# A scan beside two expert layers on one core: load queue in block order, scan input loaded twice, delta one tile sooner

## The chip, the cores and the metric

One core of a Trainium2 chip runs the whole program. The metric is the device time of one execution in microseconds. Before the change it is 2816.26 us, the median of three runs (2815.76, 2816.26 and 2824.55 us).

## The reference

The input x is (2, 2048, 1024) in float32, so 4096 rows of 1024 channels. Cut to what matters:

```
def ffn(x):      # 64 experts of rank 16, top 4
    vecs  = einsum('arh,bsh->bsar', A, x)
    idx   = top_k(norm(vecs), 4);  routes = one_hot(idx).sum(-2) / 4
    v     = einsum('bsa,bsar->bsr', routes, vecs)
    delta = einsum('bsa,ajr,bsr->bsj', routes, B, v)
    return x @ W.T + bias + delta
def scan(x):     # selective scan, 16 states
    xz = x @ W_xproj.T;  delta_r, B_mat, C_mat = xz[..., :128], xz[..., 128:144], xz[..., 144:]
    delta = softplus(delta_r @ W_dt.T + b_dt)
    dA, Bu = exp(delta * A), delta * B_mat * x
    h = dA * h + Bu   (over time);   y = sum(h * C_t)
    return y + x * D_param
x = x + 0.5 * ffn(layernorm(x))
x = x + scan(layernorm(x))
x = x + 0.5 * ffn(layernorm(x))
```

## The kernel before

**Units.** The rows are cut into 32 row blocks of 128. A unit is one expert layer on one row block; kind 1 is the first layer (its result also feeds the scan), kind 2 is the second layer, which first adds the scan's y. There are 64 units, 0 to 63, and every engine runs its own program through them in the same order. `plan` mixes the kinds: 0 to 13 are kind 1, then both kinds in turn, from 48 on all are kind 2. In a unit TensorE does the 128-deep products of W (`base`), B (`routed`) and, for the next unit, A (`experts`). VectorE picks the experts, adds up and does the scan; ScalarE does the copies, the norms and the exponentials. In this text a unit begins where VectorE starts the MAX8 of line 1095.

**The scan beside it.** The scan is cut into 64 tiles of 128 channels by 512 time steps, or of 256 channels by 256 time steps where the chunk has two row blocks, in chunks of 4, 4, 8, 8, 8, 8, 8, 8, 4 and 4 tiles. A tile has 4 groups, a group has 4 blocks, so a tile has 16 blocks and there are 1024. One block is one ACTIVATE Exp on ScalarE (`decay`, line 934, writes pA, two buffers) and one TENSOR_TENSOR_SCAN on VectorE (line 1147). GpSimd multiplies each group by B before its scan (`times_b`, lines 506 and 512, two groups ahead of the scan) and by C behind it (`times_c`, line 522). TensorE sums the states (`sum_states`, line 721), and VectorE adds x times D (`sum_up`, line 1157). Units 3 to 59 carry 17 or 18 blocks each. `scans(lo, hi)` and `decays(lo, hi)` place them in the unit in twentieths; ScalarE's decays stand two blocks ahead.

**Delta.** For each tile TensorE makes z (`z`, line 702), ScalarE the softplus (lines 888 to 898), VectorE adds and multiplies by the scan's input x in xt (`delta`, lines 1128 and 1133), and ScalarE writes delta and delta times x to DRAM (line 912). `zs` of a unit says at which of three positions this stands. From DRAM the SP queue spreads both over the partitions, 512 KB in each of four transfers for a tile: `spread_inputs` (line 360) brings delta times x, halves 0 and 1, into Ur, for `times_b`; `spread_delta` (line 353) brings delta, halves 0 and 1, into Dr, for `decay`. Both rings hold three halves. Block n = 2 of a tile is the first that reads half 1 of Dr.

**The SP queue.** SP issues every load and store but those of line 912, in program order, and a wait of one holds all behind it. In a unit (`unit`, lines 430 to 470) the order is: `slot` 0, the tile load `load_tile` of position 0 (line 390), the load of the next unit's x (line 341), the store of the scan input (442), the two DMA transposes of `turn` (403), `slot` 1 and 2, `load_tile` of position 1, the stores of ranks and B, C (450, 451), `slot` 3 and 4, `load_y` (335) and the store of the result (466). A slot is a group. At the third group of tile t the slot has `store_tile(t - 1)`, which waits for `sum_up`, then both halves of `spread_inputs(t + 1)` and half 0 of `spread_delta(t + 1)`; at the fourth group it has half 1 of `spread_delta(t + 1)`. xt has three slots; a tile's x stays there from its load until y, written in its place, is stored. `load_tile(t)` waits for the store of tile t - 3. z of tile t stands six groups before the tile's own.

Of the kernel before, what the change touches and what calls it, by code (L numbers as in the profile page):

```python
# [4 lines left out]
P = 128  # L5
# [50 lines left out]
def plan(NF, CH):  # L56

    NGRP = CH[-1].group1
    NSL = NGRP + 3
    chunk_of_row = [c for c in CH for _ in range(c.rows)]  # L60
    first_tile = {c.tile0: c for c in CH}
    slot_unit, first = {}, 0
    for u in range(SCAN0, SCAN1):
        last = (u + 1 - SCAN0) * NGRP // (SCAN1 - SCAN0)
        for n in range(first, last):
            slot_unit[n] = (u, n - first)
        first = last
# [24 lines left out]

    NTL = CH[-1].tile1
    prev = (0, 0)
    for t in range(NTL):
        s = 4 * t - 6
        u, i = slot_unit[s] if s >= 0 else (SCAN0 - 1, 3)
        at = (SCAN0 - 1, 2) if t == 0 else (u, 0) if i == 0 else (u, 1) if i < 3 else (u + 1, 0)
        assert at > prev, (t, at, prev)
        if t in first_tile:  # L100
            f = f1_at[first_tile[t].row1 - 1]
            assert at[0] >= f + 2 or (at[0] == f + 1 and at[1] == 2), (t, at, f)
        us[at[0]].zs[at[1]] = t
        prev = at
    f1s = f2s = zs = 0
    for a, b in zip(us, us[1:] + [None]):
        a.after = b
        f1s += a.kind == 1
        f2s += a.kind == 2
        zs += len(a.zs)  # L110
        a.f1s, a.f2s, a.z_end = f1s, f2s, zs
    return us


def build(nc, x, AT, BT, WT, bias, WxT, WdtT, b_dt, A_log, D_par, out):
# [41 lines left out]
    with ctx:  # L157
# [107 lines left out]

        s_ldr = sem("s_ldr")
        s_ldb = [sem(f"s_ldb{n}") for n in range(4)]; s_ldc = [sem(f"s_ldc{n}") for n in range(4)]
        s_ldt = [sem(f"s_ldt{n}") for n in range(NXT)]; s_sty = [sem(f"s_sty{n}") for n in range(NXT)]
        s_ldd = [sem(f"s_ldd{n}") for n in range(NPR)]; s_ldu = [sem(f"s_ldu{n}") for n in range(NPR)]
        s_z = sem("s_z"); s_l = sem("s_l"); s_du = sem("s_du"); s_dc = sem("s_dc")  # L270
        s_dA = sem("s_dA"); s_sc = sem("s_sc"); s_sv = sem("s_sv"); s_bm = sem("s_bm"); s_cm = sem("s_cm")
# [10 lines left out]

            return 16 * (channels_at(i // 16) + part) + i % 16

        def rows_of(t):

            return xt[:, t % NXT, :].rearrange("p (u k t) -> p k u t", k=chunk_of_tile[t].parts, t=P)

        def split(a, c):

            return a.rearrange("p (k t) -> p k t", t=c.width)

        def slot_of(a, n):
            return a.slots[n] if n < len(a.slots) else None

        def block_at(a, twentieths):

# [3 lines left out]
        def _(sp):  # L301
# [26 lines left out]
            def load_y(b, a):  # L328
                if b.kind == 2:
                    row = b.v * P  # L330
                    sp.wait_ge(s_out, a.u * 2 + 2)
                    for n in range(NXT):
                        sp.wait_ge(s_sty[n], 16 * len(range(n, chunk_of_row[b.v].tile1, NXT)))
                    src = yT_d[row:row + P, :].rearrange("p (k t) -> p k t", t=P)
                    sp.dma_start(auxy, src).then_inc(s_ldy, 16)

# [44 lines left out]
                c, k = chunk_of_tile[t], channels_at(t)  # L381
                return d[:, c.row0:c.row1, k:k + c.parts, :].rearrange("p u k t -> p u (k t)")

            def tile_of(t):
                return xt[:, t % NXT, :].rearrange("p (u n) -> p u n", u=chunk_of_tile[t].rows)

            def load_tile(t):
                sp.wait_ge(s_stn, 16 * chunk_of_tile[t].row1)
                sp.wait_ge(s_sty[t % NXT], 16 * (t // NXT))
                sp.dma_start(tile_of(t), blocks_of(xnT_u, t)).then_inc(s_ldt[t % NXT], 16)  # L390

            def store_tile(t):
                sp.wait_ge(s_y, t + 1)
                sp.dma_start(blocks_of(yT_u, t), tile_of(t)).then_inc(s_sty[t % NXT], 16)

            def turn(a, y_done):

# [4 lines left out]
                    src = un2[:, part, :, :].rearrange("p k q -> p (k q)")  # L402
                    sp.dma_start_transpose(uT[:, part, :, :], src).then_inc(s_uc[part], 16)

            def slot(a, n):
                G = slot_of(a, n)
                if G is None:
                    return
                t = G // 4 + 1
                if G % 4 == 2:  # L410
                    if t >= 2:
                        store_tile(t - 2)
                    if t < NGRP // 4:
                        spread_inputs(t, 0)
                        spread_inputs(t, 1)
                        spread_delta(t, 0)
                if G % 4 == 3 and t < NGRP // 4:
                    spread_delta(t, 1)
                for c in CH[1:]:
                    if c.group0 - 4 <= G < c.group0:  # L420
                        spread_b(c, G - c.group0 + 4)
                    if c.group0 - 2 <= G < c.group0 + 2:
                        spread_c(c, G - c.group0 + 2)
# [5 lines left out]

            def unit(l, a, b):  # L430
                late = l if l and l.kind == 1 else None
                if 0 not in a.zs:
                    ranks_due(a, 1)
                slot(a, 0)
                if 0 in a.zs:
                    load_tile(a.zs[0])
                    ranks_due(a, 1)
                if b:
                    load_x(b, a)
                if late:  # L440
                    sp.wait_ge(s_nc, late.w * 2 + 2)
                    sp.dma_start(xnT_d[late.w * P:(late.w + 1) * P, :], auxs[:, :]).then_inc(s_stn, 16)
                turn(a, a.f2s + (b is not None and b.kind == 2))
                slot(a, 1)
                slot(a, 2)
                if 1 in a.zs:
                    load_tile(a.zs[1])
                if late:
                    sp.wait_ge(s_pc, late.w + 1)
# [8 lines left out]
                slot(a, 3)  # L458
                slot(a, 4)
                if b:  # L460
                    ranks_due(b, 0)
# [558 lines left out]
        def _(dve):  # L1020
# [102 lines left out]
            def delta(a, pos):  # L1123
                if pos not in a.zs:
# [5 lines left out]
                dve.wait_ge(s_ldt[t % NXT], 16 * (t // NXT + 1))  # L1130
                c = chunk_of_tile[t]
                by_rows = "p (k u t) -> p k u t"
                V.tensor_tensor(dd[:, 1, :].rearrange(by_rows, k=c.parts, t=P), pz.rearrange(by_rows, k=c.parts, t=P),
                                rows_of(t), ALU.mult).then_inc(s_du, 1)

            def scan(i):
                G, s = i // 4, i % 4
# [159 lines left out]
```

## Time and profile before

| | |
|---|---|
| median of three runs | 2816.26 us |
| profiled execution, its own time | 2817.88 us |
| its span in the profile | 2816.1 us |
| PE busy | 2600.7 us (92%) |
| POOL busy | 2349.3 us (83%) |
| DVE busy | 2221.5 us (79%) |
| ACT busy | 1497.5 us (53%) |
| moved by DMA | 373.50 MB, 133 GB/s |

PE is TensorE, PEld its weight loads, DVE is VectorE, ACT is ScalarE, POOL is GpSimd, SP is the queue that issues most DMAs; a q behind an engine's name is its sequencer. Busy is the time in which an engine has an instruction in work. The idle time before an instruction is put down to what released it, written `<-`. DMA times run from issue to landing.

### The profile page before, as it was taken

The numbers are of one execution on the slowest core, as the hardware profiler recorded it, in microseconds if no ns is written. First come the engines' busy times: TensorE is split into PE (matmuls) and PEld (weight loads), VectorE is DVE, ScalarE is ACT, GpSimd is POOL, SyncE is SP. The second block draws the span as 40 slices with busy tenths as digits, with TensorE's granted clock in tenths as the row PEclk, the third lists the DMA queues.
The fourth block names the chain that finished last, engine by engine and source line by source line (L and its number), as shares of the span: only waits on it lengthen the run. The fifth ranks groups of instructions, "written<-read, shape, count | busy, mean of one in ns | idle before, by whom it ended". The sixth has DMA issues, their size and how long they took to land.

```text
span 2816.1 us, 39802 instructions
## 1 busy us (share of the span) xinstructions
PE 2600.7 (92%) x13597; PEld 1177.0 (42%) x13664; DVE 2221.5 (79%) x2933; ACT 1497.5 (53%) x3363; POOL 2349.3 (83%) x703
## 2 busy tenths in 40 slices
PE   4988999999999999999999999999999998889999
PEld 1444444444344443444444434444344443444444
DVE  8447888888788887888878878788788887888843
ACT  5346666665555645556455555565555554655521
POOL 2138889989899898998999999999899999989910
PEclk8999999999999999999999999999999999999999
DMA  5144434544354443544544445444455434454321
GB/s 218 48 116 136 142 118 135 163 144 138 108 159 143 133 138 109 159 144 128 143 138 132 144 138 160 133 127 131 145 156 157 143 117 138 131 147 139 92 63 53
DMA packets 303520, 373.50 MB, mean 133 GB/s; under 512 B 148435, under 2 KB 220243, under 8 KB 303318
## 3 DMA queue, kind: packets, MB, share of 16 engines
q1 hardware_dynamic: 286422, 337.40, 40.2%
q10 hardware_dynamic: 16896, 33.56, 4.0%
q8 instruction: 108, 1.77, 0.3%
q14 instruction: 94, 0.77, 0.1%
HBM read 234.05 MB, written 103.29 MB: 120 GB/s over the span
## 4 chain that ended last, share of the span: by engine, by line
PE 24%; DVE 18%; ACT 5%; DMA 5%; DVEq 4%; issue 4%; SPq 1%; ACTq 1%; POOL 1%; POOLq 0%
DVE mreg L1147 10%; PE pv L554 8%; PE po L554 5%; PE pv L558 4%; PE po L558 3%; ACT pA L934 2%; PE py L721 2%; DMA delta_scratch<-mreg 2%; DVE pv L1108 1%; DVE sel L1105 1%; DVEq L1113 1%; DMA mreg<-xnT_scratch 1%; DVEq L1107 1%; DMA xin<-x_scratch 1%; DVE xin L1071 1%
## 5 line engine op out<-in xcount | busy, mean ns | idle before, releaser
L522 POOL TENSOR_TENSOR mreg<-mreg 128x2048 f32<-128x2048 f32 x256 | 1161.6, 4538 | 48.8 <-ACT hst L920 48.7
L1147 DVE TENSOR_TENSOR_SCAN mreg<-pA,hst,mreg 128x512 f32<-128x512 f32 (+1 forms) x1024 | 1043.8, 1066 | 103.0 <-ACT pA L934 72.9
L512 POOL TENSOR_TENSOR mreg<-mreg 128x1024 f32<-128x1024 f32 x340 | 795.4, 2364 | 234.1 <-DMA mreg<-delta_scratch 229.9
L934 ACT ACTIVATE pA<-mreg,nA 128x512 f32<-128x512 f32 (+1 forms) x1280 | 738.3, 596 | 452.6 <-DVE mreg L1147 403.3
L554 PE MATMUL pv<-wA,xT 128*128 128x512 f16 x2016 | 463.8, 382 | 52.3 <-ACT xT L841 41.7
L554 PE MATMUL po<-wB,uT 128*128 128x512 f16 x2016 | 470.4, 380 | 10.2 <-DVE xin L1071 7.2
L554 PE MATMUL po<-wW,xT 128*128 128x512 f16 x2016 | 470.9, 381 | 3.6 <-issue 0.2
L506 POOL TENSOR_TENSOR mreg<-mreg 128x2048 f32<-128x2048 f32 x86 | 390.0, 4535 | 2.0 <-issue 2.0
L554 PEld LDWEIGHTS pv<-wA,xT 128*128 128x128 f16 x2016 | 191.8, 98 | 335.7 <-ACT xT L841 90.2
L554 PEld LDWEIGHTS po<-wB,uT 128*128 128x128 f16 x2016 | 191.8, 98 | 273.3 <-issue 47.0
L554 PEld LDWEIGHTS po<-wW,xT 128*128 128x128 f16 x2016 | 196.0, 98 | 238.3 <-issue 24.8
L721 PE MATMUL py<-mreg,Em 128*32 128x512 f32 (+1 forms) x2560 | 274.6, 519 | 10.4 <-DVE mreg L1157 7.8
L1089 DVE TENSOR_REDUCE n<-sel 128x32 f32<-128x512 f32 x128 | 86.2, 674 | 236.8 <-ACT sel L849 236.7
L1147 DVE TENSOR_TENSOR_SCAN mreg<-pA,cst,mreg 128x256 f32<-128x256 f32 (+1 forms) x256 | 243.1, 999 | 21.1 <-ACT pA L934 18.0
L558 PE MATMUL pv<-wA,xT 128*128 128x512 f16 x1008 | 242.9, 385 | 17.4 <-DVE xT L1085 17.4
L558 PE MATMUL po<-wB,uT 128*128 128x512 f16 x1008 | 241.1, 382 | 0.0
L558 PE MATMUL po<-wW,xT 128*128 128x512 f16 x1008 | 238.7, 380 | 0.0
L849 ACT ACTIVATE sel<-pv 128x512 f32<-128x512 f32 x128 | 75.8, 593 | 203.4 <-PE pv L558 199.3
L558 PEld LDWEIGHTS pv<-wA,xT 128*128 128x128 f16 x1008 | 97.7, 99 | 148.3 <-issue 36.6
L558 PEld LDWEIGHTS po<-wW,xT 128*128 128x128 f16 x1008 | 96.5, 98 | 133.3 <-issue 21.3
L558 PEld LDWEIGHTS po<-wB,uT 128*128 128x128 f16 x1008 | 97.1, 99 | 125.6 <-issue 25.4
L1121 DVE SCALAR_TENSOR_TENSOR xin<-po,sc,xin 128x512 f32<-128x512 f32 x128 | 92.4, 722 | 59.9 <-PE po L558 56.7
(132 smaller groups left out, 2376.0 us busy)
## 6 DMA issues: line engine op xcount, KB each, us to landing
mreg<-delta_scratch SPq DMA_DIRECT2D x256, 512.0 KB, 5.9
delta_scratch<-mreg ACTq DMA_DIRECT2D x128, 256.0 KB
xin<-x SPq DMA_DIRECT2D x32, 512.0 KB, 3.6
x_scratch<-xin SPq DMA_DIRECT2D x32, 512.0 KB, 6.1
xnT_scratch<-auxs SPq DMA_DIRECT2D x32, 512.0 KB, 2.9
mreg<-xnT_scratch SPq DMA_DIRECT2D x64, 256.0 KB, 6.7
yT_scratch<-mreg SPq DMA_DIRECT2D x64, 256.0 KB, 2.5
uT<-yT_scratch SPq DMA_DIRECT2D x32, 512.0 KB, 4.5
```

Of the source, the lines that this page charges most:

```text
L506: pool.tensor_tensor(h, u, b.broadcast_to([P, 4 * c.parts, c.width]), ALU.mult).then_inc(s_bm, 2)
L512: pool.tensor_tensor(h[:, half * n:half * n + n, :], u, b.broadcast_to([P, n, c.width]), ALU.mult).then_inc(s_bm, 1)
L522: pool.tensor_tensor(h, h, by_c, ALU.mult).then_inc(s_cm, 1)
L554: last = nc.tensor.matmul(dst, lhs[:, 0, k, :], w[:, wb, k, nb * HF:(nb + 1) * HF], start=(first and k == 0 and wb == 0), stop=False)
L558: last = nc.tensor.matmul(dst, lhs[:, 1, k, :], w[:, 0, k, nb * HF:(nb + 1) * HF], start=False, stop=(stop and k == KD - 1))
L721: last = nc.tensor.matmul(split(py[32 * s:32 * s + 32, :], c)[:, n, :], Em[:, :], h[:, c.parts * s + n, :], start=(g == 0 and n == 0), sto ...
L849: nc.scalar.activation(sel[:, nb * HF:(nb + 1) * HF], pv[:, nb, :], ACT.Square).then_inc(s_sq, 1)
L934: last = nc.scalar.activation(dst[:, part, :], src[:, part, :], ACT.Exp, scale=nA[:, m:m + 1])
L1071: V.tensor_tensor(dst, pty[half], dst, ALU.add).then_inc(s_ya, 1)
L1089: V.tensor_reduce(n2[:, nb * NE // 2:(nb + 1) * NE // 2], sel3[:, nb * NE // 2:(nb + 1) * NE // 2, :], AX.X, ALU.add)
L1121: V.scalar_tensor_tensor(dst, po[:, nb, :], sc[:, 3:4], dst, ALU.mult, ALU.add).then_inc(s_res, 1)
L1147: last = V.tensor_tensor_scan(h, split(pA[:, i % 2, :], c)[:, part, :], h, before, ALU.mult, ALU.add)
```

## The change

Three things change. (1) SP's slots become `loads(a, lo, hi)`, which goes through the scan's blocks of a stretch of the unit in twentieths: 0 to 2 at the unit's start, 2 to 9 behind `turn` and the tile load of position 1, 9 to 18 behind the stores of ranks, 18 to 20 behind the store of the result. With n the block's number in tile t, `spread_inputs(t + 1)` stands at n = 6 (half 0) and 7 (half 1), `store_tile(t - 1)` and half 0 of `spread_delta(t + 1)` at 9, and half 1 at 15. (2) `load_tile` fills two slots of xt for delta alone and waits for delta of tile t - 2; `load_again(t)`, at n = 13, loads the same 256 KB into the third slot, in which y is formed and stored. It waits for the store of tile t - 1, and `sum_up` waits for it. (3) z of tile t stands ten groups ahead in place of six (`AHEAD`), and `load_tile` of position 0 goes to the end of the unit before. Two deltas stand in units 3, 5, 9, 12, 20, 28, 36, 44 and 52 in place of 3, 12, 20, 28, 36, 44 and 52; none in 8 and 58.

```diff
+AHEAD = 10
...
-        s = 4 * t - 6
+        s = 4 * t - AHEAD
...
+        at = (u, 0) if i == 0 else (u, 1) if i < 3 else (u + 1, 0)
         if t in first_tile:
-            f = f1_at[first_tile[t].row1 - 1]
-            assert at[0] >= f + 2 or (at[0] == f + 1 and at[1] == 2), (t, at, f)
+            at = max(at, (f1_at[first_tile[t].row1 - 1] + 2, 0))
+        if at <= prev:
+            at = (prev[0], 1) if prev[1] == 0 else (prev[0] + 1, 0)
...
             def load_tile(t):
                 sp.wait_ge(s_stn, 16 * chunk_of_tile[t].row1)
-                sp.wait_ge(s_sty[t % NXT], 16 * (t // NXT))
-                sp.dma_start(tile_of(t), blocks_of(xnT_u, t)).then_inc(s_ldt[t % NXT], 16)
+                sp.wait_ge(s_du, max(t - NXT + 2, 0))
+                slot = t % (NXT - 1)
+                sp.dma_start(tile_of(slot, t), blocks_of(xnT_u, t)).then_inc(s_ldt[slot], 16)
+
+            def load_again(t):
+                sp.wait_ge(s_sty, 16 * t)
+                sp.dma_start(tile_of(NXT - 1, t), blocks_of(xnT_u, t)).then_inc(s_ldv, 16)
...
+            def loads(a, lo, hi):
+                if a.u < SCAN0 or a.u > SCAN1:
+                    return
+                for i in range(block_at(a, lo), block_at(a, hi)):
+                    t, n = i // 16, i % 16
+                    if n == 6 and t + 1 < NTL:
+                        spread_inputs(t + 1, 0)
+                    if n == 7 and t + 1 < NTL:
+                        spread_inputs(t + 1, 1)
+                    if n == 9 and t >= 1:
+                        store_tile(t - 1)
+                    if n == 9 and t + 1 < NTL:
+                        spread_delta(t + 1, 0)
+                    if n == 13 and t < NTL:
+                        load_again(t)
+                    if n == 15 and t + 1 < NTL:
+                        spread_delta(t + 1, 1)
+                    ...
...
-                slot(a, 1)
-                slot(a, 2)
                 if 1 in a.zs:
                     load_tile(a.zs[1])
+                loads(a, 2, 9)
...
                 sp.dma_start(dst, xin[:, a.p, :]).then_inc(s_stx[a.p], 16)
+                loads(a, 18, 20)
+                if b and 0 in b.zs:
+                    ranks_due(b, 0)
+                    load_tile(b.zs[0])
...
             def sum_up(t):
                 dve.wait_ge(s_e, 4 * t + 4)
+                dve.wait_ge(s_ldv, 16 * (t + 1))
```

## Rows read from the trace of the kernel before

**Rows 1.** Waits of POOL, 280 to 2680 us: total, times, longest.

```profile
POOL mreg L512 <- DMA mreg<-delta_scratch: 122.8, 35, 10.5
```

**Rows 2.** Waits of DVE, the same stretch.

```profile
DVE mreg L1147 <- ACT pA L934: 87.7, 83, 3.8
DVE mreg L1133 <- DMA mreg<-xnT_scratch: 24.6, 6, 4.6
...
DVE mreg L1147 <- POOL mreg L512: 8.5, 5, 2.4
```

**Rows 3.** Waits of the SP queue, the same stretch.

```profile
SPq L394 <- DVE mreg L1157: 361.5, 49, 20.4
...
SPq L360 <- DMA delta_scratch<-mreg: 83.5, 19, 8.9
```

**Rows 4.** Windows, units 12, 17, 23, 24, 25, 33, 52 and 10 to 52: engines' busy time.

```profile
588.39:635.74 47.35, 44.00 (x231) 20.33 (x231) 37.02 (x46) 28.71 (x62) 41.02 (x14) 1.00 0.42 129
...
812.54:859.09 46.55, 40.69 (x197) 17.32 (x197) 36.98 (x45) 24.14 (x53) 44.56 (x16) 0.96 0.53 148
...
1076.82:1123.54 46.72, 40.66 (x206) 16.62 (x205) 37.85 (x46) 24.02 (x53) 36.21 (x11) 1.00 0.40 118
1123.54:1168.76 45.22, 42.84 (x216) 19.64 (x214) 34.45 (x40) 22.44 (x47) 44.63 (x14) 0.96 0.74 193
1168.76:1211.03 42.27, 39.45 (x198) 16.51 (x197) 36.99 (x46) 24.15 (x53) 42.27 (x15) 1.00 0.39 124
...
1517.25:1559.00 41.75, 41.41 (x220) 19.04 (x214) 34.58 (x40) 22.84 (x48) 41.75 (x15) 1.00 0.50 155
...
2331.99:2380.10 48.11, 41.55 (x203) 18.11 (x203) 37.04 (x46) 25.35 (x55) 42.54 (x14) 0.96 0.46 133
504.67:2380.10 1875.43, 1769.22 (x9017) 783.09 (x9054) 1547.66 (x1852) 1029.00 (x2200) 1753.04 (x515) 0.99 0.47 139
```

The columns are start:end and length in us, then busy us (with the number of instructions) of PE, PEld, DVE, ACT and POOL, the granted clock, the DMA share and GB/s.

**Rows 5.** Timeline of unit 36 (from 1642.59): SP queue and DVE; start, us.

```profile
1669.13 1.18 SPq L360 DMA_DIRECT2D mreg<-delta_scratch  x2
...
1671.05 0.54 SPq L390 DMA_DIRECT2D mreg<-xnT_scratch  x1
...
1678.70 0.69 DVE L1133 TENSOR_TENSOR mreg<-pv,mreg 128x512 f32<-128x512 f32 x1 [4.54 <-DMA mreg<-xnT_scratch]
```

**Rows 6.** Timeline of unit 23 (from 1076.82): SP queue and POOL.

```profile
1090.16 1.19 SPq L360 DMA_DIRECT2D mreg<-delta_scratch  x2
...
1095.72 4.66 POOL L512 TENSOR_TENSOR mreg<-mreg 128x1024 f32<-128x1024 f32 x2 [10.51 <-DMA mreg<-delta_scratch]
```

**Rows 7.** Timeline of unit 17 (from 812.54): SP queue, ACT, DVE.

```profile
824.70 0.55 SPq L353 DMA_DIRECT2D mreg<-delta_scratch  x1
...
832.13 0.69 ACT L934 ACTIVATE pA<-mreg,nA 128x512 f32<-128x512 f32 x1 [5.32 <-DMA mreg<-delta_scratch]
...
832.85 2.46 DVE L1147 TENSOR_TENSOR_SCAN mreg<-pA,hst,mreg 128x512 f32<-128x512 f32 x2 [3.33 <-ACT pA L934]
```

**Rows 8.** Timeline of unit 25 (from 1168.76): SP queue and ACT.

```profile
1180.92 0.55 SPq L353 DMA_DIRECT2D mreg<-delta_scratch  x1
...
1185.21 0.69 ACT L934 ACTIVATE pA<-mreg,nA 128x512 f32<-128x512 f32 x1 [2.18 <-DMA mreg<-delta_scratch]
```

**Rows 9.** Timeline of unit 26 (from 1211.03): SP queue and DVE.

```profile
1209.18 0.51 SPq L353 DMA_DIRECT2D mreg<-delta_scratch  x1
...
1218.31 2.83 SPq L403 DMA_TRANSPOSE uT<-sel  x2
...
1219.78 4.80 DVE L1147 TENSOR_TENSOR_SCAN mreg<-pA,hst,mreg 128x512 f32<-128x512 f32 x4
```

**Rows 10.** Timeline of unit 34 (from 1559.00): SP queue and DVE.

```profile
1568.31 2.64 SPq L403 DMA_TRANSPOSE uT<-sel  x2
...
1574.71 2.45 DVE L1147 TENSOR_TENSOR_SCAN mreg<-pA,cst,mreg 128x512 f32<-128x512 f32 x2
```

**Rows 11.** The page's DMA issues: KB each, us to landing.

```profile
mreg<-xnT_scratch SPq DMA_DIRECT2D x64, 256.0 KB, 6.7
```

More of the change, by code:

```diff
@@ L95, in plan @@
     for t in range(NTL):
-        s = 4 * t - 6
+        s = 4 * t - AHEAD
         u, i = slot_unit[s] if s >= 0 else (SCAN0 - 1, 3)
-        at = (SCAN0 - 1, 2) if t == 0 else (u, 0) if i == 0 else (u, 1) if i < 3 else (u + 1, 0)
-        assert at > prev, (t, at, prev)
+        at = (u, 0) if i == 0 else (u, 1) if i < 3 else (u + 1, 0)
         if t in first_tile:
-            f = f1_at[first_tile[t].row1 - 1]
-            assert at[0] >= f + 2 or (at[0] == f + 1 and at[1] == 2), (t, at, f)
+            at = max(at, (f1_at[first_tile[t].row1 - 1] + 2, 0))
+        if at <= prev:
+            at = (prev[0], 1) if prev[1] == 0 else (prev[0] + 1, 0)
+        if t == 0:
+            at = (SCAN0 - 1, 2)
+            assert f1_at[first_tile[0].row1 - 1] + 1 == at[0]
+        u, i = slot_unit[max(4 * t - 6, 0)]
+        assert t < 2 or at <= ((u, 0) if i == 0 else (u, 1) if i < 3 else (u + 1, 0)), (t, at)
         us[at[0]].zs[at[1]] = t
@@ L267, in build @@
         s_ldb = [sem(f"s_ldb{n}") for n in range(4)]; s_ldc = [sem(f"s_ldc{n}") for n in range(4)]
-        s_ldt = [sem(f"s_ldt{n}") for n in range(NXT)]; s_sty = [sem(f"s_sty{n}") for n in range(NXT)]
+        s_ldt = [sem(f"s_ldt{n}") for n in range(NXT - 1)]; s_ldv = sem("s_ldv"); s_sty = sem("s_sty")
         s_ldd = [sem(f"s_ldd{n}") for n in range(NPR)]; s_ldu = [sem(f"s_ldu{n}") for n in range(NPR)]
@@ L283, in column, with by_part @@
             return 16 * (channels_at(i // 16) + part) + i % 16
-        def rows_of(t):
-            return xt[:, t % NXT, :].rearrange("p (u k t) -> p k u t", k=chunk_of_tile[t].parts, t=P)
+        def by_part(slot, t):
+            return xt[:, slot, :].rearrange("p (u k t) -> p k u t", k=chunk_of_tile[t].parts, t=P)
         def split(a, c):
             return a.rearrange("p (k t) -> p k t", t=c.width)
-        def slot_of(a, n):
-            return a.slots[n] if n < len(a.slots) else None
         def block_at(a, twentieths):
@@ L331, in load_y @@
                     sp.wait_ge(s_out, a.u * 2 + 2)
-                    for n in range(NXT):
-                        sp.wait_ge(s_sty[n], 16 * len(range(n, chunk_of_row[b.v].tile1, NXT)))
+                    sp.wait_ge(s_sty, 16 * chunk_of_row[b.v].tile1)
                     src = yT_d[row:row + P, :].rearrange("p (k t) -> p k t", t=P)
@@ L382, in blocks_of, with tile_of @@
                 return d[:, c.row0:c.row1, k:k + c.parts, :].rearrange("p u k t -> p u (k t)")
-            def tile_of(t):
-                return xt[:, t % NXT, :].rearrange("p (u n) -> p u n", u=chunk_of_tile[t].rows)
+            def tile_of(slot, t):
+                return xt[:, slot, :].rearrange("p (u n) -> p u n", u=chunk_of_tile[t].rows)
             def load_tile(t):
                 sp.wait_ge(s_stn, 16 * chunk_of_tile[t].row1)
-                sp.wait_ge(s_sty[t % NXT], 16 * (t // NXT))
-                sp.dma_start(tile_of(t), blocks_of(xnT_u, t)).then_inc(s_ldt[t % NXT], 16)
+                sp.wait_ge(s_du, max(t - NXT + 2, 0))
[4 more added lines that the diff above has]
+                sp.dma_start(tile_of(NXT - 1, t), blocks_of(xnT_u, t)).then_inc(s_ldv, 16)
             def store_tile(t):
                 sp.wait_ge(s_y, t + 1)
-                sp.dma_start(blocks_of(yT_u, t), tile_of(t)).then_inc(s_sty[t % NXT], 16)
+                sp.dma_start(blocks_of(yT_u, t), tile_of(NXT - 1, t)).then_inc(s_sty, 16)
             def turn(a, y_done):
@@ L403, in turn @@
                     sp.dma_start_transpose(uT[:, part, :, :], src).then_inc(s_uc[part], 16)
-            def slot(a, n):
-                G = slot_of(a, n)
-                if G is None:
+            def loads(a, lo, hi):
+                if a.u < SCAN0 or a.u > SCAN1:
                     return
[L409 to L423, printed above, removed]
+                for i in range(block_at(a, lo), block_at(a, hi)):
[12 more added lines that the diff above has]
+                        spread_delta(t + 1, 1)
+                    for c in CH[1:]:
+                        if n % 4 == 0 and c.group0 - 4 <= i // 4 < c.group0:
+                            spread_b(c, i // 4 - c.group0 + 4)
+                        if n % 4 == 0 and c.group0 - 2 <= i // 4 < c.group0 + 2:
+                            spread_c(c, i // 4 - c.group0 + 2)
             def ranks_due(a, pos):
@@ L431, in unit @@
                 late = l if l and l.kind == 1 else None
[L432 to L437, printed above, removed]
+                ranks_due(a, 1)
+                loads(a, 0, 2)
                 if b:
@@ L457, in unit @@
                         spread_c(CH[0], g)
[L458 to L461, printed above, removed]
+                loads(a, 9, 18)
                 if b and b.after:
@@ L1129, in delta @@
                 dve.drain()
-                dve.wait_ge(s_ldt[t % NXT], 16 * (t // NXT + 1))
+                slot = t % (NXT - 1)
+                dve.wait_ge(s_ldt[slot], 16 * (t // (NXT - 1) + 1))
                 c = chunk_of_tile[t]
@@ L1133, in delta @@
                 V.tensor_tensor(dd[:, 1, :].rearrange(by_rows, k=c.parts, t=P), pz.rearrange(by_rows, k=c.parts, t=P),
-                                rows_of(t), ALU.mult).then_inc(s_du, 1)
+                                by_part(slot, t), ALU.mult).then_inc(s_du, 1)
             def scan(i):
@@ L1152, in sum_up @@
                 dve.wait_ge(s_e, 4 * t + 4)
+                dve.wait_ge(s_ldv, 16 * (t + 1))
                 c, k = chunk_of_tile[t], channels_at(t)
                 for n in range(c.parts):
-                    x_n = rows_of(t)[:, n, :, :]
+                    x_n = by_part(NXT - 1, t)[:, n, :, :]
                     y_n = split(py[:, :], c)[:, n, :].rearrange("p (u t) -> p u t", t=P)
```

## The prediction

> **What bounds the kernel now.** I looked at the waits first, then cut the trace into units with windows, then read the timelines of the units that are too long.
>
> The waits of POOL show what the change aims at. In 280 to 2680 us it stands 122.8 us, in 35 waits, for the tile of delta times x that `spread_inputs` brings [rows 1]. But POOL's lag hardly reaches anybody: DVE waits 8.5 us for the halves it makes, against 87.7 us for ACT's pA and 24.6 us, in 6 waits of about 4 us, for the scan input of `load_tile` [rows 2]. So the 122.8 us are no forecast of the gain. The waits of SP say why the data come late: the store of y holds the queue for 361.5 us in 49 waits, with the input spreads right behind it, and the landing of delta in DRAM for 83.5 us [rows 3].
>
> The windows give the unit's floor. Unit 33 takes 41.75 us with PE busy 41.41 and POOL 41.75 [rows 4]: both are full, a unit cannot go far below that. Units 10 to 52 take 1875.43 us [rows 4]; 43 times 41.75 is 1795, so 80 us is the excess of the middle part over its floor, and that, with little at both ends, is all that better feeding can win. Where it sits: six units with two deltas (12, 20, 28, 36, 44, 52; the first and last take 47.35 and 48.11 us), some 36 us; unit 23 (46.72), and 15 like it; 17 (46.55); 24 (45.22) [rows 4]. These are some 55 of the 80 us; the other 25 are spread thinly.
>
> **The change part by part.**
>
> *Tile load of units with two deltas.* In unit 36 the load for the second delta is issued at 1671.05, right behind the input spreads of 1669.13, which had waited for the first delta's landing; DVE then stands 4.54 us at line 1133, between the two halves of the split of x that PE's next products need [rows 5]. After, that load stands right behind the turn, some 16 us sooner, it waits only for a delta of the unit before, and the spreads wait for a delta that is a tile older. The 4.5 us go. The unit's excess is 5.6 to 6.4 us [rows 4]; the rest is the second delta's own work, which stays. Bounds: nothing (something else ends last) to all 6.0 us. I take 4.3 us, the nearest row, for six units: -26 us. Unit 3 has the same wait: -3 us. Units 5 and 9 now have two deltas, 8 and 58 none: I take +2 us (0 to +4).
>
> *Input spreads ahead of the store of y.* In unit 23 they are issued at 13.3 us, behind turn and store, and POOL stands 10.51 us [rows 6]. After, they stand at n = 6 and 7, which for this tile is the end of unit 22 and the start of 23: 12 us sooner. POOL's wait goes, and half 0 of delta has two 512 KB transfers fewer ahead of it. Unit 23 is 5.0 us over the floor, 15 the same, 7, 31 and 55 less. I take -12 us for the five (0 to -15). Everywhere else POOL's wait goes without gain, since unit 33's length is PE's too.
>
> *Crowding at a chunk's start.* In unit 17 the half 1 of delta lands 7.4 us after its issue, in unit 25 after 4.3 us [rows 7, 8], and ACT stands 5.32 against 2.18 us. Their lengths differ by 4.3 us [rows 4] for 3.1 us of wait: such a stall goes into the unit's length in full, up to 1.4 times. After, part of the B and C loads stand before the turn and the spreads in the unit before. I take -4.5 us for 17 and 24 together (0 to -8).
>
> *Half 1 of delta at n = 15.* This one speaks against the change. Before, it stood at the fourth group, n = 12. For seven tiles, 8, 17, 26, 35, 44, 53 and 62, that was the queue's first place of unit 10, 18, 26, 34, 42, 50, 58; n = 15 is the unit's third or fourth block, and so falls behind the turn. In unit 26 it was issued at 1209.18 and the turn ends at 1221.14 [rows 9]. So: issue at 1221.2, landing 4.3 us later [rows 8] at 1225.5, decay 0.7 us [rows 7], scan at 1226.2. The fourth of the four scans from 1219.78 now starts at 1223.4 [rows 9]. That is 2.8 us late, and there is no slack in front. With up to 1.4 times, 3.2 us for each of 10, 18 and 26: +9.5 us. In unit 34 the turn ends at 1570.95 and the scan of that block starts at 1574.71 [rows 10]; by the same steps it starts at 1576.0, 1.3 us late, 1.5 us for each of 34, 42, 50 and 58: +6 us. Bounds: 0, if the landing is hidden, and with unit 17's 7.4 us of landing 3.1 us more in each of seven, times 1.4: +45 us.
>
> *The second load.* 64 issues of 0.54 us [rows 5] on a queue that mostly waits cost nothing by themselves; `sum_up` comes 11 blocks (over 25 us) behind it, so its landing of 6.7 us [rows 11] is covered. It adds 64 times 256 KB, 17 MB on 373.5. But it stands ahead of half 1 of delta behind the turn in units 9, 17, 25, 49 and 57, where that half is just in time: 0.6 us of issue and about as much of transfer, +3 us (0 to +8). Its wait for the store of y just before holds the queue 2 to 6 us; behind it only the half at n = 15 is due, in its own time.
> The Trainium skill, "DMA: Bandwidth & Descriptors", "Queues, rings and completion order", says more: a transfer's semaphore increment lands only after every earlier write of that DMA engine. By that, with the 6.7 us, the half of delta would land 6.1 us after its issue where a second load is ahead, and the sum would be some 4 us higher; the second tile load of row 1671.05 lands behind three 512 KB transfers, so its time says little for a lone one.
>
> *Small ones.* of the 25 us spread thinly I give -3 us (0 to -10) to waits of the queue that reach DVE through POOL or ACT.
>
> The sum: -26 -3 +2 -12 -4.5 +9.5 +6 +3 -3 = -28 us on the profiled execution's 2817.9 us, so 2790; the median of before is 1.6 us lower, hence 2788 us.
>
> **The rivals.**
>
> *A. All feeding stalls go and the late half of delta is hidden.* Then units 10 to 52 come near the floor: two-delta units keep 1.5 us each for their own work, and of the 25 us spread thinly 15 stay, as more than half of the units have a floor of their own by their kind. 80 - 9 - 15 is 56, with 5 at the ends 61: 2755 us. For it: PE and POOL both full in unit 33. Against it: ACT has no lead at n = 2 in unit 26. Chance 0.20.
>
> *B. Off the path.* The two-delta units stay at 47 to 48 us because the second delta's own work (two more DVE passes, five of ACT, in a unit whose order is fixed) takes the place of the wait. Then -26 and -3 fall away and the sum is +1: 2817 us by the median, within 0.3%. For it: PE is busy 44.00 us in unit 12, 2.6 more than in 33 [rows 4]. Against: in unit 52 it is only 41.55. Chance 0.14.
>
> *C. Slower: half 1 of delta is late by a crowded landing.* It now follows turn, and in several units the store of the scan input and the second load; if it lands as in unit 17, 7.4 us after issue, the seven units lose 45 us in place of 15, and 9, 17, 25, 49, 57 some 4 us each in place of 0.6: +47 against the sum, 2835 us. It decides from a landing of about 6 us on. For it: DMA is busy 0.53 of the time in unit 17, 0.39 in 25. Against it: in the units at issue nothing but the transposes precedes. Chance 0.12.
>
> *D. The forecast*, 2768 to 2806 us by its own terms. Chance 0.54.
>
> **How the numbers follow.** A measurement of this kernel tells about 0.3%, 8.4 us, from no change. A and D are faster, 0.74, less 0.01 for the edge of D: faster 0.73, same 0.15, slower 0.12. The range reaches to A's centre and to B's: 2752 to 2816 us.
>
> **What would show it.** Right: line 1133 waits for no tile load; POOL waits under 40 us for the spreads; unit 12, 20, ... 52 take 43 to 44.5 us; unit 23 under 44; units 10, 18 and 26 are 3 us longer than before with a wait of line 934 on the spread of delta. Wrong: two-delta units at 47 us (B); line 934 waiting over 60 us in all for the spreads (C); units 10 to 52 under 1820 us (A). The forecast also fails if SP is held somewhere new, so that the load of x at line 341 or the turn comes later than about 7 or 10 us into a unit.

## The result, and the profile after it

The changed kernel is slower by about 1%: 2849.47 us median of 4 runs (2844.37 to 2857.12) against 2818.18 us before (now of four runs), a ratio of 1.0114, 95% interval [1.0097, 1.0132]. The prediction of 2788 us missed in size and in sign, and the range with it. The profiled execution took 2844.37 us with a span of 2842.5, 26.4 us over the span of before.

First the waits of four engines in 280 to 2680 us (total, times, longest), to be laid beside [rows 1 to 3]. POOL:

```profile
POOL mreg L529 <- ACT hst L927: 120.3, 73, 4.2
...
POOL mreg L519 <- DMA mreg<-delta_scratch: 14.0, 9, 3.9
```

DVE:

```profile
DVE mreg L1155 <- ACT pA L941: 110.7, 97, 3.7
DVE xT L1092 <- ACT xT L848: 42.0, 50, 4.1
DVE pv L1135 <- ACT pv L905: 26.8, 18, 4.7
```

ACT:

```profile
ACT pA L941 <- DMA mreg<-delta_scratch: 53.0, 19, 5.3
ACT mreg L895 <- DMA delta_scratch<-mreg: 20.7, 8, 3.6
```

The SP queue, in the row of the second load:

```profile
SPq L397 <- DMA yT_scratch<-mreg: 148.6, 35, 9.4
```

Both waits that the change aimed at are gone. POOL waits 14.0 us for the spreads in place of 122.8 [rows 1], and no row of DVE names a tile load, where 24.6 us stood [rows 2]. But POOL's idle time has only moved: it now waits 120.3 us for `hst`, which ScalarE copies from the scan's output, where it waited 39.0 us before. And two new waits are ACT's. One is line 895, for the first delta's way into DRAM, 20.7 us (1.3 us in the kernel before). The other is line 941, for the spread of delta, 53.0 us (36.8 before), with 26.8 us of DVE at line 1135 behind it (15.9 before). SP is also held somewhere new: its longest wait is now 453.2 us in 50 waits for POOL, ahead of an input spread. That is not what costs the 26 us: in e9, which is faster than the kernel before, it is still 432.7 us.

The windows say in which units that counts (start:end, length, then busy us of PE, PEld, DVE, ACT, POOL, granted clock, DMA share, GB/s). They are units 12, 23, 24, 25, 26, 28, 34, 52 and 10 to 52, against [rows 4]:

```profile
596.15:644.31 48.16, 44.60 (x226) 20.05 (x225) 37.19 (x45) 28.61 (x62) 44.42 (x14) 0.96 0.51 139
...
1086.21:1128.84 42.63, 39.09 (x198) 16.59 (x197) 37.67 (x46) 24.02 (x53) 40.82 (x13) 1.00 0.48 147
1128.84:1171.36 42.52, 42.23 (x224) 19.20 (x223) 34.45 (x41) 22.70 (x47) 39.69 (x12) 1.00 0.65 184
1171.36:1218.06 46.70, 40.69 (x198) 17.33 (x197) 37.10 (x46) 24.26 (x53) 41.08 (x15) 0.96 0.46 141
1218.06:1262.47 44.41, 42.72 (x224) 19.02 (x223) 34.42 (x40) 22.42 (x47) 41.57 (x12) 1.00 0.49 149
1304.28:1353.49 49.21, 44.68 (x226) 20.11 (x225) 35.79 (x43) 25.55 (x52) 42.90 (x13) 0.97 0.44 130
...
1565.89:1613.35 47.46, 41.59 (x203) 17.91 (x205) 37.04 (x46) 24.18 (x52) 42.12 (x12) 0.93 0.44 131
...
2357.78:2406.66 48.88, 42.72 (x204) 18.46 (x203) 37.05 (x46) 25.43 (x55) 42.13 (x13) 0.93 0.48 140
510.20:2406.66 1896.46, 1782.73 (x9069) 788.38 (x9068) 1548.94 (x1852) 1028.47 (x2202) 1756.00 (x515) 0.98 0.49 144
```

Units 23 and 24 fell to the floor as forecast. Units 12, 28 and 52, with two deltas, did not fall at all. Units 25, 26 and 34 rose, 34 from 41.8 to 47.46 us. Units 10 to 52 together take 1896.46 us, 21 more than before [rows 4]. Cut this way over all units, the profile's 26.5 us are made up as follows (lengths after less lengths before, summed over each class).

| class of units | forecast | after | e1 | e9 | e12 |
|---|---|---|---|---|---|
| two deltas: 12, 20, 28, 36, 44, 52 | -26 | +2.5 | +8.0 | -17.2 | -18.0 |
| unit 3 | -3 | +1.7 | -3.7 | -2.8 | -2.7 |
| 5, 8, 9 (deltas changed places) | +2 | +7.7 | +6.6 | +9.9 | +3.3 |
| input spreads sooner: 7, 15, 23, 31, 55 | -12 | -13.6 | -9.6 | -9.9 | -7.0 |
| chunk starts 17, 24 | -4.5 | -4.4 | -5.6 | -5.0 | -6.3 |
| half 1 late: 10, 18, 26 | +9.5 | +6.4 | -0.2 | -0.1 | -0.8 |
| half 1 late: 34, 42, 50, 58 | +6 | +17.7 | -2.2 | -2.2 | -2.3 |
| second load ahead of the half: 25, 49, 57 | +3 | +5.4 | +0.3 | +0.4 | -1.0 |
| all others, and the time before unit 0 | -3 | +3.1 | +2.5 | +0.4 | -2.7 |
| sum | -28 | +26.5 | -3.9 | -26.4 | -37.5 |

### The profile page after: what moved, and what is told of

It reads as the page before. It is cut to its first block, busy times and chain, and to the rows that moved or that the text cites. A ratio compares the mean times of both kernels' runs of the same rounds, so it can differ in the third digit from the quotient of the medians.

```text
span 2842.5 us, 39965 instructions
## 1 busy us (share of the span) xinstructions
PE 2620.4 (92%) x13664; PEld 1183.3 (42%) x13664; DVE 2223.2 (78%) x2933; ACT 1496.9 (53%) x3363; POOL 2350.5 (83%) x703
## 3 DMA queue, kind: packets, MB, share of 16 engines
q1 hardware_dynamic: 316118, 354.18, 41.8%
## 4 chain that ended last, share of the span: by engine, by line
PE 41%; DVE 25%; ACT 10%; DMA 8%; DVEq 6%; issue 6%; ACTq 2%; SPq 1%; POOL 1%; POOLq 0%
PE pv L561 14%; DVE mreg L1155 13%; PE po L561 8%; PE pv L565 7%; PE po L565 5%; DMA delta_scratch<-mreg 4%; ACT pA L941 3%; PE py L728 3%; DMA mreg<-delta_scratch 3%; DVE pv L1115 2%; DVE sel L1112 2%; DVEq L1120 2%; PE pv L690 2%; DVEq L1114 1%; ACT xT L848 1%
```

## The experiments

### e1: half 1 of delta back at n = 12

```
-  if n == 13 and t < NTL: load_again(t)
-  if n == 15 and t + 1 < NTL: spread_delta(t + 1, 1)
+  if n == 12 and t + 1 < NTL: spread_delta(t + 1, 1)
+  if n == 13 and t < NTL: load_again(t)
```

> The changed kernel with one move: half 1 of the delta spread stands at n = 12, ahead of the second load, in place of n = 15. Theory (the late half costs the most): in units 10, 18, 26, 34, 42, 50 and 58 that half was issued behind the turn, ACT waited 3.4 to 5.3 us for it and the units grew by 1 to 6 us, 24 us in all, with 4 us more in unit 25; it goes back to the queue's place before the turn, so the time falls by 24 to 30 us, from 1.011 to about 1.001 of before (2820 us), and the seven units return to 42 us (43 for 58). Units with two deltas stay at 47 to 49 us. Rival (the queue is held by its wait for POOL, 453 us in 50 waits at line 362, or by the wait for the store of y): the half's place in the program does not matter, the time stays above 2840 us.

Measured: 2805.93 us, 0.9964 [0.9952, 0.9976] of before, 43.5 us under the changed kernel by the medians, 30.4 by the profiled spans (the profile of e1 is of the slowest of its ten runs, that of the changed kernel of the fastest of its four). In the profile (span 2812.1) units 34, 42 and 50 are back at 41.8, 41.8 and 41.1 us, and 25 at 42.2. This one position turned the change from a gain into a loss. The six units with two deltas stay long and even grow by another 5.5 us in all (its windows stand under e9), so that part of the miss is not here.

### e8: the softplus ahead of the decays

In unit 34 of the changed kernel (start, duration; in brackets the idle time before it and what ended it) the half is issued behind the turn and lands as forecast, but look at what stands behind the decay:

```profile
1575.20 2.66 SPq L410 DMA_TRANSPOSE uT<-sel  x2
...
1577.96 0.55 SPq L355 DMA_DIRECT2D mreg<-delta_scratch  x1
...
1582.49 0.69 ACT L941 ACTIVATE pA<-mreg,nA 128x512 f32<-128x512 f32 x1 [4.88 <-DMA mreg<-delta_scratch]
1583.26 0.63 ACT L903 ACTIVATE mreg<-mreg 128x512 f32<-128x512 f32 x1
1583.96 0.60 ACT L905 ACTIVATE pv<-mreg 128x512 f32<-128x512 f32 x1
...
1584.59 0.70 DVE L1135 TENSOR_TENSOR pv<-pv,mreg 128x512 f32<-128x512 f32 x1 [4.27 <-ACT pv L905]
...
1585.97 3.62 DVE L1155 TENSOR_TENSOR_SCAN mreg<-pA,cst,mreg 128x512 f32<-128x512 f32 x3
```

ACT's order has this tile's softplus (lines 903 and 905) behind the late decay, and DVE's has its two delta operations ahead of the scan. So the decay, done at 1583.2, is not what the scan waits for: DVE stands 4.27 us for the softplus and the scan starts at 1585.97, 20.1 us into the unit. The forecast had 17.0 (1576.0 in a unit that began at 1559.00 [rows 10]).

```
-  decays(4, 7)
   softplus(a, 0)
+  decays(4, 7)
```

> The changed kernel, half 1 at n = 15 as it is, with ScalarE's softplus of position 0 ahead of the three or four decays that stand before it. Theory (in units 34, 42 and 50 DVE can run on through its scans but stands 4 to 4.7 us at line 1135 for the softplus, which stands on ACT behind the decay that waits for the late half): these three units fall from 47 us to 43.5 us or less, line 1135 waits no longer for pv in them, and the whole is 8 to 12 us faster than the changed kernel, near 1.008 of before. Rival (the late decay holds the scan itself, as it does in units 10, 18 and 26): units 34, 42 and 50 stay at 47 us.

Measured: 2838.27 us, 1.0051 [1.0032, 1.0069]. That is 11.2 us under the changed kernel by the medians, as expected, 6.1 us by the profiled spans, and 0.6% by the ratios, each to its own runs of the kernel before. Units 34, 42 and 50 fell to 44.6, 44.4 and 43.6 us, not quite to the 43.5 expected. The half is as late as before, and the wait at 1135 is gone. The same place of unit 34 in e8:

```profile
1579.38 0.55 SPq L355 DMA_DIRECT2D mreg<-delta_scratch  x1
...
1584.04 1.30 ACT L941 ACTIVATE pA<-mreg,nA 128x512 f32<-128x512 f32 x2 [5.01 <-DMA mreg<-delta_scratch]
1584.77 3.63 DVE L1155 TENSOR_TENSOR_SCAN mreg<-pA,cst,mreg 128x512 f32<-128x512 f32 x3 [1.66 <-ACT pA L941]
```

The scan now waits 1.66 us for the decay alone and starts 17.5 us into the unit; the unit takes 44.63 us, and the four units of its class lose 8.9 us to the kernel before in place of 17.7. Half of that class's loss was the softplus in the queue behind the decay.

### e5 and e4: the parts done alone on the kernel before

e5 takes half 1 of delta out of the fourth slot of the kernel before and issues it at n = 15:

```
-  if G % 4 == 3 and t < NGRP // 4: spread_delta(t, 1)
...
+  def late_half(a, lo, hi):
...
+      for i in range(block_at(a, lo), block_at(a, hi)):
+          if i % 16 == 15 and i // 16 + 1 < NGRP // 4: spread_delta(i // 16 + 1, 1)
...
+  late_half(a, 0, 2)
...
+  late_half(a, 2, 9)
...
+  late_half(a, 9, 18)
...
+  late_half(a, 18, 20)
```

> The kernel before with half 1 of the delta spread alone at n = 15, in the four places in which the changed queue has it; nothing else. Theory (the late half is the whole loss): units 10, 18, 26, 34, 42, 50 and 58 grow as in the changed kernel (44.4, 44.4, 44.4, 47.5, 47.2, 47.0, 44.3 us), 24 to 30 us in all, 1.009 to 1.011 of before. Rival (only together with the second load ahead of it, or with the input spread's wait for POOL, is the half late): under 8 us.

Measured: 2910.47 us, 1.0311 [1.0293, 1.0330], 90 us slower and three times what was expected. The direction shows that the late half is harmful by itself, without the rest of the change. The size says little of the changed kernel: of the 92 us between the profiled spans, 35.6 are in the seven units 10, 18, 26, 34, 42, 50 and 58 (24.1 in the changed kernel), and 41.7 in units 7, 15, 23, 31 and 55. In unit 23 the half stands behind a load of B, which waits 8.4 us for POOL, and is issued 33.2 us into the unit. That unit takes 59.9 us, ACT standing in it:

```profile
1137.45 1.30 ACT L943 ACTIVATE pA<-mreg,nA 128x512 f32<-128x512 f32 x2 [12.08 <-DMA mreg<-delta_scratch]
```

e4 adds to the kernel before only the second load, into the slot of its own:

```
+  def load_again(t):
+      sp.wait_ge(s_sty, 16 * t)
+      sp.dma_start(tile_of(NXT - 1, t), blocks_of(xnT_u, t)).then_inc(s_ldv, 16)
...
   if G % 4 == 3 and t < NGRP // 4: spread_delta(t, 1)
+  if G % 4 == 3 and t <= NGRP // 4: load_again(t - 1)
```

> The kernel before with the second load alone: two slots for delta, a third loaded again at the tile's fourth group behind half 1 of the delta spread; queue order and AHEAD as before. Theory: 17 MB more and a wait for the store of y right before cost little: 1.000 of before, within 6 us either way. Rival (the second load is what costs: its wait for the store of y holds the queue, 150 us in 36 waits in the changed kernel, and its transfer takes the DMA engines): 10 to 25 us slower than before.

Measured: 2812.37 us, 0.9984 [0.9970, 0.9997]: behind half 1 of delta, as it stands here, the second load costs nothing. In the changed kernel's unit 25 it stands ahead of the late half. The half was issued at 1184.16 and ACT waited:

```profile
1183.48 0.57 SPq L397 DMA_DIRECT2D mreg<-xnT_scratch  x1
...
1184.16 0.53 SPq L355 DMA_DIRECT2D mreg<-delta_scratch  x1
1184.79 0.54 SPq L362 DMA_DIRECT2D mreg<-delta_scratch  x1
...
1191.14 0.69 ACT L941 ACTIVATE pA<-mreg,nA 128x512 f32<-128x512 f32 x1 [5.25 <-DMA mreg<-delta_scratch]
```

That is 7.0 us from issue to decay, against 4.3 us in the same unit before [rows 8]. The Trainium skill, "DMA: Bandwidth & Descriptors", "Queues, rings and completion order", says that a transfer's semaphore increment lands only after every earlier write of that DMA engine; by it the prediction had worked out 6.1 us, from a second load that takes 6.7 us to land. The trace does not bear this working out. The second load lands 3.2 us after its issue at 1183.48, as the view of DMA issues in 1183.4 to 1183.6 shows (KB, us to landing):

```profile
mreg<-xnT_scratch SPq DMA_DIRECT2D x1, 256.0 KB, 3.2
```

That is at 1186.7, 4.5 us ahead of the half's own landing, so the order of the two can't have held the half. The load may still have slowed it. In units 34, 42, 50 and 58, where SP issues an input spread 0.6 us behind the half as here (line 362) and no second load ahead of it, the half lands after 4.3 to 4.9 us; in 49 and 57, with both, after 5.3 and 5.5 us, in 25 after 7.0. No run moves the second load alone, so how it costs this, and why 25 most, stays open.

### e3: AHEAD = 6, delta no longer a tile sooner

```
-AHEAD = 10
+AHEAD = 6
```

> The changed kernel with AHEAD = 6 in place of 10: z and delta stand where they stood before, the queue order and the second load are kept. Theory (late half and crowded write): the seven late halves stay, +24 us; in the units with two deltas the spreads wait again for the landing of the delta, so nothing crowds its write, while the tile load is no longer behind them: these seven units take 44 to 45.5 us in place of 48, 20 us less: 2830 us, 1.004 of before. Rival (the shift of delta is harmless or helps): 2849 us or more, since the queue waits again for delta (83 us before).

Measured: 2837.11 us, 1.0070 [1.0051, 1.0090], 0.4% under the changed kernel. What it told was more than its time: units 20, 28 and 36 fell to 44.4, 45.1 and 43.6 us, with the second delta's work as before. So that work doesn't hold these three; 12, 44 and 52 stayed at 47.3 to 48.6 us. What differs is SP, which here stands 562.9 us for the landing of delta, and so issues nothing beside that write: in all six units it lands after 8.6 to 8.9 us, and line 895 waits 0.3 us. So it is the earlier delta, the third part of the change, that freed SP from this wait. In 12 and 52 ACT waits 5.8 and 10.0 us in all for the spread of delta; what holds 44 was not settled.

### e2 and e7: which transfer crowds the write

In the six units 12 to 52 with two deltas the write of the first delta landed 8.7 to 9.4 us after its issue before, 10.9 to 12.2 us after the change, and 11.3 to 13.9 us in e1. Two transfers issued beside it were put off, one at a time. e2 is e1 with half 0 of delta at n = 11:

```
-  if n == 9 and t + 1 < NTL: spread_delta(t + 1, 0)
+  if n == 11 and t + 1 < NTL: spread_delta(t + 1, 0)
```

> As the kernel before it, and half 0 of the delta spread stands at n = 11 in place of 9. Theory (in a unit with two deltas the first delta's write to DRAM lands 11.3 us after its issue in place of 8 because this 512 KB spread and the store of y are issued right behind it, and ACT stands for it at line 895 with the copy to xT behind): the write lands 2 to 3 us sooner, line 895 waits under 8 us in all in place of 20.7, and the nine units with two deltas lose 2 to 3.5 us each: about 20 us less than the kernel with half 1 at 12 alone, near 0.994 of before (2800 us). Rival (the store of y, or the second half of the input spread at n = 7, crowds it, or the second delta's own work fills the unit): the units with two deltas stay at 47 to 49 us and the time is that of the kernel with half 1 at 12 within 4 us.

Measured: 2810.44 us, 0.9984 [0.9971, 0.9997]; about 20 us less than e1 had been expected and none came. The six units take 6.5 us more than before the change, the write lands after 11.4 to 13.2 us, and line 895 waits 23.5 us. e7 is e1 with the store of y at n = 11, behind half 0:

```
-  if n == 9 and t >= 1: store_tile(t - 1)
+  if n == (11 if t < NTL else 9) and t >= 1: store_tile(t - 1)
```

> The changed kernel with half 1 of the delta spread at n = 12, and the store of y at n = 11 in place of 9. Theory (what crowds the first delta's write in a unit with two deltas is the store of y, issued within 1 us of it and landing after 11 us itself): the write lands 2 to 3 us sooner after its issue, line 895 waits under 8 us in all in place of 21.7, the units with two deltas take 44 to 46 us, 15 to 25 us less than with half 1 at 12 alone, about 0.990 of before. Rival (the input spread's halves just before it crowd it): the units stay at 47 to 51 us, and the time within 4 us of the kernel with half 1 at 12 alone.

Measured: 2810.80 us, 0.9962 [0.9949, 0.9974], as e1 and not the 0.990 of the theory; line 895 waits 24.9 us and the write lands after 12.2 to 12.7 us. Neither is the crowd alone.

### e9: nothing issued beside the write

e9 is e1 with one wait more:

```
   if 1 in a.zs:
       load_tile(a.zs[1])
+      if 0 in a.zs:
+          sp.wait_ge(s_std, 32 * (a.zs[0] + 1))
   loads(a, 2, 9)
```

> Kernel e1 (half 1 of delta at n = 12) with one wait more: in the nine units with two deltas (3, 5, 9, 12, 20, 28, 36, 44, 52) SP stands, right behind turn and tile load, until the first delta has landed in DRAM. Everything that it issued in that stretch (the second input spread, the store of y, half 0 of delta) comes behind the landing. Theory: these transfers beside the write make it late, and ACT's line 895 waits for it. Then the write lands 8.6 to 9.5 us after its issue as in the kernel before (11.3 to 13.9 in e1), line 895 waits under 4 us in all (21.7 in e1), the units 12, 20, 28, 36, 44, 52 take 43.5 to 45 us in place of 47 to 52, and the time is some 25 us under e1's, 2780 us, a ratio of 0.986 to 0.990. Rival 1 (the second delta's own work holds these units, B of the prediction): the wait at 895 goes and the units stay at 47 us or more; 0.995 to 0.997. Rival 2 (the transfers put off are now late themselves): new waits of POOL or ACT for the spreads in the second half of these units, 46 us or more, 0.994 to 1.000. Rival 3 (the write is slow by itself, whoever runs beside it): it still lands 11 us or later and nothing changes.

Measured: 2789.9 us, 0.9893 [0.9877, 0.9910], the write lands after 8.7 to 9.2 us again, and ACT waits for it (line 897 here) 2.8 us in all. Unit 28 is where to see it. In the kernel before, SP issued nothing from 1313.2 to 1322.1, and ACT hardly waited:

```profile
1313.35 0.54 ACTq L912 DMA_DIRECT2D delta_scratch<-mreg  x1
...
1322.09 1.18 SPq L360 DMA_DIRECT2D mreg<-delta_scratch  x2
...
1322.16 0.69 ACT L888 ACTIVATE mreg<-pv,bdt 128x512 f32<-128x512 f32 x1 [0.36 <-DMA delta_scratch<-mreg]
```

After the change SP issues an input spread, the store of y and half 0 of delta (and two small stores between them) within 3 us around the write, and the wait travels from ACT's line 895 over the copy to xT behind it to DVE and PE:

```profile
1321.25 0.51 SPq L362 DMA_DIRECT2D mreg<-delta_scratch  x1
...
1322.42 0.55 ACTq L919 DMA_DIRECT2D delta_scratch<-mreg  x1
...
1323.11 0.67 SPq L401 DMA_DIRECT2D yT_scratch<-mreg  x1
...
1323.89 1.23 SPq L355 DMA_DIRECT2D mreg<-delta_scratch  x1
...
1334.43 0.69 ACT L895 ACTIVATE mreg<-pv,bdt 128x512 f32<-128x512 f32 x1 [3.56 <-DMA delta_scratch<-mreg]
...
1336.82 0.69 DVE L1092 TENSOR_TENSOR xT<-pv,xT 128x512 f16<-128x512 f32 x1 [4.07 <-ACT xT L848]
...
1338.74 1.61 PE L561 MATMUL pv<-wA,xT 128*128 128x512 f16 x5 [4.53 <-ACT xT L848]
```

In e9 SP issues nothing beside the same write. It lands after 8.7 us, and what was put off is issued after it. The last two lines show the price of the hold, POOL and ACT waiting for the spreads that were put off:

```profile
1305.37 0.53 ACTq L921 DMA_DIRECT2D delta_scratch<-mreg  x1
...
1314.05 1.49 SPq L362 DMA_DIRECT2D mreg<-delta_scratch  x2
1314.12 0.69 ACT L897 ACTIVATE mreg<-pv,bdt 128x512 f32<-128x512 f32 x1 [0.30 <-DMA delta_scratch<-mreg]
...
1318.92 2.35 POOL L521 TENSOR_TENSOR mreg<-mreg 128x1024 f32<-128x1024 f32 x1 [8.01 <-DMA mreg<-delta_scratch]
...
1323.69 0.69 ACT L943 ACTIVATE pA<-mreg,nA 128x512 f32<-128x512 f32 x1 [4.74 <-DMA mreg<-delta_scratch]
```

The windows of e1 for units 28, 34 and 10 to 52:

```profile
1293.33:1341.93 48.60, 44.67 (x226) 20.03 (x225) 35.80 (x42) 25.55 (x52) 42.89 (x13) 0.96 0.45 131
...
1555.14:1596.98 41.84, 39.76 (x203) 16.88 (x205) 36.82 (x46) 24.27 (x52) 41.05 (x12) 1.00 0.48 141
...
504.59:2379.16 1874.57, 1775.66 (x9059) 784.99 (x9052) 1548.02 (x1853) 1029.71 (x2202) 1755.28 (x515) 0.99 0.50 147
```

and of e9 for 28, 52 and 10 to 52:

```profile
1287.22:1332.83 45.61, 43.17 (x226) 19.58 (x225) 35.88 (x42) 25.54 (x52) 35.41 (x12) 1.00 0.44 125
...
2312.39:2355.93 43.54, 40.30 (x205) 17.79 (x203) 37.03 (x46) 25.25 (x55) 36.05 (x12) 1.00 0.45 135
508.43:2355.93 1847.50, 1760.45 (x9060) 780.60 (x9052) 1548.30 (x1852) 1029.03 (x2202) 1747.72 (x514) 1.00 0.51 148
```

Units with two deltas fall by 2.9 to 5.9 us against e1, to 43.5 us (52) up to 47.4 (12); units 10 to 52 take 1847.50 us in place of 1874.57. The theory stands, and the second delta's own work (rival B's reason) does not hold these units at 47 us, with unit 12 left open: it takes what it took before the change. Rival 2 is seen as well. POOL waits 61.2 us for the spreads (11.3 in e1) and ACT 38.8 (11.3 in e1). In unit 12 ACT waits 5.1 us for its spread and the scan 3.3 us behind it. Unit 5 even rose to 53.8 us, where POOL waited up to 12.4 us for a spread.

### e10 and e12: the best of these edits together

e10 is e9 with the softplus ahead, as in e8.

> Kernel e9 with softplus(a, 0) ahead of decays(4, 7) on ACT, as in e8. If the softplus behind a decay still holds VectorE's delta here (line 1135 waited 15.0 us in e1), that wait goes and the time falls by 2 to 8 us under e9's. If not, the decays behind the softplus come later by its 2 us and the time rises by 0 to 8 us. I take 3 us less than e9: 2777 us, 0.986. Both theories leave the landing of the delta write as in e9.

Measured: 2785.5 us, 0.9877 [0.9863, 0.9892], 4.4 us under e9 where 3 were expected. The slowest of its four runs, 2787.33 us, is under the fastest of e9, 2789.38, but the two ratio intervals overlap, so the gain is likely and not firmly shown. e12 is e10 without the hold in units 3 and 5:

```
-  if 0 in a.zs:
+  if 0 in a.zs and a.u > 5:
```

> Kernel e10 with the hold of SP left out in units 3 and 5, kept in 9, 12, 20, 28, 36, 44 and 52. In e9 and e10 unit 5 took 53.8 and 54.1 us, against 49.2 in e1 without the hold: there three stores of the early units and both input spreads stand behind it, and POOL waits up to 12.4 us for the spread. If the hold is the cause, unit 5 falls to about 49 us and the time to 2780 us, a ratio of 0.985 to 0.987. If unit 5 is long for another reason, it stays at 54 us and the time within 2 us of e10, 2785.5 us.

Measured: 2781.02 us, 0.9860 [0.9838, 0.9882]. Unit 5 fell from 54.1 to 47.8 us, so the hold had made it long; unit 3 rose by 1.5. e12 beats both kernels, the one before by 1.4%, the changed one by some 2.5% (0.9860 over 1.0114).

## Why the prediction was wrong, step by step

**Tile load of units with two deltas: the step that failed** (-26 us taken, +2.5 measured, and unit 3 with -3 against +1.7). The wait at line 1133 went as said. The step priced the stall that goes and named for its successor only "the second delta's own work". It counted it as a help that the spreads now wait for a delta that is a tile older, and did not ask what SP, freed from its wait for the landing [rows 3], would then issue beside that same write. Its wait had been a shield: without it the write landed after 10.9 to 12.2 us in place of 8.7 to 9.4 (e3, e9), and ACT's line 895 with DVE and PE behind it waited for that. By e9 the step is worth -17 us once the shield is back, 2.9 us a unit in place of 4.3; a part of the rest is the price of the hold. Rival B had nearly the right lengths (47 to 48 us, measured 47.0 to 49.2) for a reason that e3 and e9 speak against; no rival had the write's landing.

**Half 1 of delta at n = 15: the sign was right, the size was not** (+15.5 taken, +24.1 measured). The issue behind the turn, 4.5 us to the decay in unit 34, and for 10, 18 and 26 a scan late by some 3 us are as forecast; those three cost 6.4 us in place of 9.5. The miss is units 34, 42 and 50, 5.4 to 5.6 us each in place of 1.5. There the step counted the decay and the scan, and left out the softplus behind the decay on ACT and DVE's delta ahead of the scan. e8 shows about half of it, and e1 all of it. Rival C's total, 2835 us, was the nearest, but by luck: its cause, a landing of 7.4 us in these seven units, did not occur. It was 4.1 to 4.9 us there, and 7.0 us in unit 25 alone.

**The second load.** +3 us taken, +5.4 in units 25, 49 and 57 (by e1 nearly all of it goes with the late half's place), and as much of unit 9's 4.6 us as is due to the same order. The sign was right: with the load ahead the half landed 0.4 to 2.7 us later than in units without it. The working by the 6.7 us of [rows 11] was not: the load itself lands after 3.2 us in unit 25. e4 shows that the load costs nothing where nothing due stands behind it. It waits 148.6 us for the store of y, which now takes 5.7 us to land at the median instead of 2.5; no run shows a cost of that.

**Units 5, 8, 9:** +2 taken, +7.7 measured. Units 5 and 9 became units with two deltas, and such a unit is long for the reason above; the step gave them the work and not the stall.

**Input spreads ahead of the store, and the chunk starts,** came out as forecast: -13.6 against -12, and -4.4 against -4.5. The reading that POOL's other waits are worth nothing fits too: they fell by some 109 us and no class but these gained.

**The others:** -3 taken, +3.1 measured, spread over 37 units and the time before unit 0; what it consists of was not looked for.

Rival A wanted units 10 to 52 under 1820 us; the lowest of all runs, e10, has 1843.95. The sum was off by 54.5 us in the profile, 33 of it by the two-delta units and unit 3, 11 by the late half and the second load, 6 by units 5, 8 and 9. What stays open is which of the transfers beside the write costs it how much, and whether it is bytes or order that makes it late. Two buffers for delta, which would have taken the wait of line 895 away without a hold, were not tried.

## What to carry to other kernels

When a queue is freed from a wait, list what it will now issue in the time it used to stand, and whose transfers are in flight then: a wait for a landing also keeps that landing quick. Price a late operand by walking every engine's order from it to the next matmul, not only its own consumer. And where a change moves several things, test each position alone before dropping it: here one line's place was 30 to 43 us, and one wait's absence another 16 to 22 (e1 to e9).

## What the runs showed of the hardware

A wait in a unit can cost more than itself. In unit 34 of the changed kernel PE stands 5.60 us for ACT's xn, and the granted clock falls from full to half, the 1.2 GHz level, while it stands, and stays there after PE has work again. Windows of 2 us from 1590 (columns as above):

```profile
1590.00:1592.00 2.00, 0.00 (x0) 0.00 (x0) 1.93 (x5) 1.03 (x5) 2.00 (x1) 1.00 0.23 75
1592.00:1594.00 2.00, 0.00 (x0) 0.00 (x0) 2.00 (x2) 1.67 (x7) 2.00 (x2) 0.52 0.26 102
1594.00:1596.00 2.00, 0.99 (x5) 0.99 (x6) 0.67 (x2) 2.00 (x3) 2.00 (x2) 0.50 0.18 69
1596.00:1598.00 2.00, 2.00 (x8) 1.15 (x7) 2.00 (x3) 1.26 (x4) 2.00 (x2) 0.50 0.39 123
1598.00:1600.00 2.00, 2.00 (x10) 0.65 (x12) 2.00 (x3) 1.37 (x3) 2.00 (x1) 0.77 0.92 285
```

For the same 203 matmuls PE is busy 41.59 us there and 39.76 in e1, where the clock stays full. So up to 1.8 of the unit's 5.6 us can be the clock's; how much of that reached the unit's length was not tested. In unit 28 PE is busy 44.68 us against 43.17 us in e9. The prediction's factor of up to 1.4 may be the same: its unit 17 ran at a clock of 0.96 with PE busy 40.69 us, unit 25 at 1.00 with 39.45 us [rows 4], 1.2 us of their difference of 4.3.

The landing of two 256 KB writes to DRAM is the other: 8.7 to 9.4 us with nothing issued beside it (before, e9), 10.9 to 13.9 us with an input spread, a store of 256 KB and a 512 KB spread issued around it (changed kernel, e1; units 12 to 52). These are issued by SP and the writes by ACT, and the DMA share of these units is only 0.40 to 0.51. A mean share of about a half does not say that a given transfer is undisturbed.
